# Spreading the C rows of a state-space layer with a float32 product in place of three bfloat16 parts

## What is computed

```
xs = silu(conv(x @ in_w[:DI]))              # DI = 256 channels, 4 taps
dt, B, C = split(xs @ xproj_w)              # rank 8, 16 states, 16 states
dt = softplus(dt @ dt_w + dt_b)
h = exp(dt * A) * h + dt * B * xs           # step by step in time, 16 states per channel
y = sum over states of h * C + D * xs
out = (y * silu(z)) @ out_w
```

## Time and profile before

| | us |
|---|---|
| median of 3 runs | 7244.17 (7243.53 to 7258.09) |
| the profiled execution | 7231.49, span 7229.6 |
| PE busy | 6436.1 (89%) |
| DVE busy | 5332.4 (74%) |
| ACT busy | 4057.1 (56%) |
| POOL busy | 2813.5 (39%) |

### The profile page before, as it was taken

How to read it: one execution, slowest core, us unless ns; L and a number is a source line. 1 busy time by engine, 2 the same in 40 slices (tenths; PEclk the granted TensorE clock), 3 DMA queues, 4 the chain that set the end, 5 groups by cost and what they waited for, 6 DMA issues and landing times. The chain is left out here.

```text
span 7229.6 us, 188705 instructions
## 1 busy us (share of the span) xinstructions
PE 6436.1 (89%) x74428; PEld 3944.6 (55%) x74428; DVE 5332.4 (74%) x8931; ACT 4057.1 (56%) x6024; POOL 2813.5 (39%) x1680
## 2 busy tenths in 40 slices
PE   7989987887797999989999789999899999989998
PEld 5767665444532333333333256666576767666676
DVE  7867576665467999999999856687577777768444
ACT  4556343665447777777777745455344444456433
POOL 3311175332216888888888501164022222221000
PEclk9999988999798999999999899999999999999999
DMA  1000000000101222222222100000000000000000
GB/s 29 0 21 12 8 6 8 3 4 2 15 0 62 76 78 76 80 75 76 73 76 75 47 12 14 22 17 3 12 2 2 2 2 2 2 16 14 1 0 23
DMA packets 115879, 190.00 MB, mean 26 GB/s; under 512 B 38661, under 2 KB 74746, under 8 KB 114970
## 3 DMA queue, kind: packets, MB, share of 16 engines
q1 hardware_dynamic: 112218, 183.47, 8.0%
q10 hardware_dynamic: 3264, 0.54, 0.1%
HBM read 173.87 MB, written 7.98 MB: 25 GB/s over the span
## 5 line engine op out<-in xcount | busy, mean ns | idle before, releaser
L2611 POOL TENSOR_TENSOR m_dBx<-m_dtx,m_Bs 128x1024 f32<-128x1024 f32 x515 | 1166.5, 2284 | 227.1 <-DVE m_hs L2976 185.0
L2976 DVE TENSOR_TENSOR_SCAN m_hs<-m_ps_dA,m_dBx 128x512 f32<-128x512 f32 x1030 | 1203.0, 1212 | 56.6 <-POOL m_dBx L2611 56.0
L2730 PE MATMUL m_ps_y<-m_yc,ident 128*128 128x512 f32 x2060 | 1021.4, 618 | 0.0
L2835 ACT ACTIVATE m_ps_dA<-m_dt,m_A 128x504 f32<-128x504 f32 x1030 | 683.3, 679 | 426.0 <-DVE m_hs L2976 423.4
L2107 POOL TENSOR_TENSOR a_s<-a_s,a_den 128x1024 f32<-128x1024 f32 x128 | 243.8, 1904 | 1123.7 <-DVE a_den L2153 1123.7
L2987 DVE TENSOR_TENSOR m_yc<-m_hs,m_ps_C 128x1024 f32<-128x1024 f32 x515 | 619.3, 1203 | 1.2 <-PE m_ps_C L2711 1.1
L2730 PEld LDWEIGHTS m_ps_y<-m_yc,ident 128*128 128x128 f32 x2060 | 350.0, 189 | 357.2 <-issue 357.2
L2711 PEld LDWEIGHTS m_ps_C<-m_parts,m_sel 48*128 48x128 bf16 x516 | 47.7, 92 | 567.7 <-DVE m_yc L2987 421.4
L2711 PE MATMUL m_ps_C<-m_parts,m_sel 48*128 48x512 bf16 x516 | 199.7, 387 | 176.4 <-DVE m_yc L2987 176.2
L636 POOL TENSOR_TENSOR c_kbd<-c_kf,c_hmask 128x1024 f32<-128x1024 f32 x66 | 125.1, 1895 | 503.0 <-ACT c_kf L545 484.9
L2151 DVE TENSOR_REDUCE a_den<-a_s 128x16 f32<-128x1024 f32 x128 | 156.1, 1219 | 207.5 <-ACT a_s L2058 207.5
(11 more groups left out here) (750 smaller groups left out, 15803.9 us busy)
## 6 DMA issues: line engine op xcount, KB each, us to landing
m_Bs<-BC_rows SPq DMA_DIRECT2D x258, 512.0 KB, 3.6
c_kvb<-in_ctxT SPq DMA_DIRECT2D x68, 128.0 KB, 2.1
c_kvb<-in_ctxT SPq DMA_DIRECT2D x17, 256.0 KB, 2.7
out_dram<-X SPq DMA_DIRECT2D x1, 4096.0 KB
BC_rows<-m_low SPq DMA_DIRECT2D x33, 64.0 KB, 2.9
part_rows<-m_split SPq DMA_DIRECT2D x33, 48.0 KB, 1.7
m_parts<-part_rows SPq DMA_DIRECT2D x33, 48.0 KB, 1.7
m_piece<-BC_rows SPq DMA_DIRECT2D x33, 32.0 KB, 1.7
```

The costliest lines, as they stand in the source:

```text
L2611: return nc.gpsimd.tensor_tensor(to, one, other, ALU.mult)
L2730: last = nc.tensor.matmul(ps_y[:, m, :], C.ident[:], of[:, m, :], start=s == 0, stop=s == NS - 1)
L2835: nc.scalar.activation(seqs(ps_dA[:, h % 3, :]), seqs(dt[:, par, m, :]), ACT.Exp, scale=A[:, second, m, s:s + 1]).then_inc(decay, 1)
L2976: nc.vector.tensor_tensor_scan(hs[:, s % HS, m, :], ps_dA[:, (2 * s + m) % 3, :], dBx[:, s % BX, m, :], 0.0, ALU.mult, ALU.add).then_inc(s ...
```

## The change

The C rows stay in SBUF in float32. The product that spreads them takes, as its weights, one column of the identity, read 128 times (a [32, 128] tile with step 0), and as its moving operand the 32 rows of B and C of the low product, which now has two buffers. `split_rows`, `sel`, `pick_row`, `piece`, `rest`, `split`, `parts`, their DMAs through DRAM and their semaphores are gone, and SP stores the 16 rows of B alone. The last pair of groups is taken out of the hardware loop: group 30 is written with PE's `fronts=1` (only one piece of convolution of the group behind group 31), and group 31 runs states 3 to 15 with no preparation of another group, then its gating, projection and addition.

```diff
-        sel = sb("sel", [P, NS, P], BF16)
...
-        low = sb("low", [P, GT])
-        parts = sb("parts", [P, 2, GT], BF16)
-        piece, rest, split = sb("piece", [P, PIECE]), sb("rest", [P, PIECE]), sb("split", [P, 3, PIECE], BF16)
+        low = sb("low", [P, 2, GT])
...
-        LOOPS = ((0, C.NG // 2 - 1), (C.NG // 2, C.NG))
+        LOOPS = ((0, C.NG // 2 - 1), (C.NG // 2, C.NG - 1))
...
-                sp.dma_start(BC_rows[par], low[0:2 * NS, :]).then_inc(rows_stored, 16)
+                sp.dma_start(BC_rows[par], low[0:NS, par, :]).then_inc(rows_stored, 16)
...
             def spread_C(j, s, par):
                 if s == 0:
-                    pe.wait_ge(parts_loaded, j * 16 + 16)
-                nc.tensor.matmul(ps_C[:], sel[0:3 * NS, s, :], parts[0:3 * NS, par, :], start=True, stop=True).then_inc(C_done, 1)
+                    pe.wait_ge(rows_low, j + 1)
+                one = bc(C.ident[0:2 * NS, NS + s:NS + s + 1], [2 * NS, P])
+                nc.tensor.matmul(ps_C[:], one, low[0:2 * NS, par, :], start=True, stop=True).then_inc(C_done, 1)
...
-            for m in range(NHF):
-                nc.tensor.matmul(ps_y[:, m, :], C.ident[:], yc[:, (AHEAD - 1) % 2, m, :], start=False, stop=True)
+            group(GROUPS - 2, 0, [1, 1, 1, 1], 1)
+            for s in range(AHEAD, NS):
+                if s == SKIPPED:
+                    skip(1, 1)
+                step(GROUPS - 1, s, 1, final=True)
+            project(GROUPS - 1, 1, True)
...
-            def split_rows(j):
-
-                dve.wait_ge(piece_loaded, j * 16 + 16)
-                nc.vector.tensor_copy(split[:, 0, :], piece[:])
-                dve.drain()
-                nc.vector.tensor_tensor(split[:, 1, :], piece[:], split[:, 0, :], ALU.subtract)
-                nc.vector.tensor_tensor(rest[:], piece[:], split[:, 0, :], ALU.subtract)
-                dve.drain()
-                nc.vector.tensor_tensor(split[:, 2, :], rest[:], split[:, 1, :], ALU.subtract).then_inc(split_ready, 1)
...
+            def final_group(i, par):
+                for s in range(AHEAD, NS):
+                    scan(i, s)
+                    weigh(i, s - 1)
+                weigh(i, NS - 1)
+                gated(i, par)
+                add_output(i, True)
```

More of the change, by code:

```diff
@@ L2592, in _ @@
                     group(pair * 2 + par, par)
[L2593 to L2596, removed]
+            for par in range(2):
+                group(GROUPS - 2 + par, par)
         n_prepared = 2
@@ L2651, in _, with group @@
                 state(0, s, 0, True)
-            with pool.Fori(0, C.NG) as pair:
-                for par in range(2):
[L2654 to L2659, removed]
+            def group(i, par):
+                for s in range(AHEAD, NS):
+                    state(i, s, par)
+                    front(i + 1, s, 1 - par)
+                for s in range(AHEAD):
+                    state(i + 1, s, 1 - par)
+            with pool.Fori(0, C.NG - 1) as pair:
+                for par in range(2):
+                    group(pair * 2 + par, par)
+            group(GROUPS - 2, 0)
+            for s in range(AHEAD, NS):
+                state(GROUPS - 1, s, 1)
         @block.tensor
@@ L2703, in step_sizes @@
                 for m in range(NHF):
-                    last = nc.tensor.matmul(bank[m][:], dt_w[rank_rows, m * P:(m + 1) * P], low[rank_rows, :], start=True,
+                    last = nc.tensor.matmul(bank[m][:], dt_w[rank_rows, m * P:(m + 1) * P], low[rank_rows, par, :], start=True,
                                             stop=True)
@@ L2717, in skip, with project @@
                     nc.tensor.matmul(ps_y[:, m, :], diagD[:, m, :], xs[:, par, m, :], start=False, stop=False)
-            def project(i, second):
+            def project(i, second, final=False):
                 pe.wait_ge(y_ready, i + 2)
-                pe.wait_ge(xs_ready, i * NHF + 5)
+                pe.wait_ge(xs_ready, i * NHF + (3 if final else 5))
                 for p in range(TPG):
@@ L2731, in add, with step @@
                 last.then_inc(y_added, 1)
-            def step(j, s, par, between=None):
+            def step(j, s, par, between=None, final=False):
                 rank = DVE_WEIGHS.index(s)
@@ L2737, in step @@
                     spread_C(j, DVE_WEIGHS[rank + 1], par)
-                else:
+                elif not final:
                     spread_C(j + 1, 0, 1 - par)
@@ L2763, in front, with group @@
                     convolve(j + 1, (s - 12) // 2, (s - 12) % 2)
-            def group(i, par, of):
+            def group(i, par, of, fronts=AHEAD):
                 for s in range(AHEAD, NS):
@@ L2772, in group @@
                 for s in range(AHEAD):
-                    front(i + 2, s, par, True, of[2], of[3])
+                    if s < fronts:
+                        front(i + 2, s, par, True, of[2], of[3])
                     step(i + 1, s, 1 - par, (lambda: project(i, of[0])) if s == 0 else None)
@@ L2865, in front @@
                         act.wait_ge(rows_stored, j * 16)
-                    nc.scalar.activation(low[0:64, :], ps_k[0:64, :], ACT.Copy).then_inc(rows_low, 1)
+                    nc.scalar.activation(low[0:64, par, :], ps_k[0:64, :], ACT.Copy).then_inc(rows_low, 1)
                 elif s == 7:
@@ L2927, in _ @@
                     group(pair * 2 + par, par, [1, 1, 1, 1])
-            front(GROUPS + 1, AHEAD, 1, True, 1, 1)
+            group(GROUPS - 2, 0, [1, 1, 1, 1])
+            for s in range(AHEAD, NS):
+                state(GROUPS - 1, s, 1, 1)
         @block.vector
@@ L3016, in group, with gated, add_output @@
                 weigh(i + 1, 1)
+                add_output(i, second)
+            def gated(i, par):
+                dve.wait_ge(y_added, i * NS + NS)
+                nc.vector.tensor_tensor(q[:], sz[:, par, :, :], ps_y[:], ALU.mult).then_inc(y_ready, 1)
+            def add_output(i, second):
                 dve.wait_ge(out_done, i + 1)
@@ L3030, in _ @@
                     group(pair * 2 + par, par, True)
-            weigh(GROUPS, AHEAD - 1)
+            group(GROUPS - 2, 0, True)
+            final_group(GROUPS - 1, 1)
 def mamba_join(C, name):
@@ L4062, in constants @@
     c["pick_mean"] = (row[:, None] // S == np.arange(2)[None, :]).astype(np.float32) / S
[L4063 to L4066, removed]
     c["flip"] = np.kron(np.eye(2, dtype=np.float32), np.eye(S, dtype=np.float32)[::-1]).astype(np.float32)
```

45 lines of the change are left out of this document (15 added, 30 removed).

## The result

The changed kernel takes 7435.26 us (median of 4 runs, 7423.72 to 7446.26), the kernel before 7243.89 in the same comparison: a ratio of 1.026, 95% interval 1.0242 to 1.0279. It is slower, and the forecast of 7437 us is 2 us away. The four runs lie at two values, 7424 and 7446; the profiled one is 7446.26 with a span of 7444.5, and why they differ is not shown, though the mean granted clock is 0.959 and 0.960 in the longer two and 0.962 in the shorter.

A forecast was written before the change was run, and what follows sets the result against it. VectorE was taken to bound the kernel, TensorE after the change: 202 (thirty intervals) + 5.8 (first group) - 14.1 (last group) - 1.2 (setup) = +193 us on 7244.2, so 7437 us; eight times in ten 7390 to 7470.

The forecast's parts named there:

- The gaps at C: TensorE around the C product: passes 0.53 us apart, addition 0.52 behind, a state 2.96, with a front 4.68.
- TensorE becomes the bound, the split buys nothing: State-space groups: TensorE needs 64.8 us against VectorE's 57.15, a group 6.75 longer; the split's 0.90 gains nothing.
- The sum of PE's group, 64.8 us: TensorE's work in one group of sixteen states: 63.9 us, plus 0.8 wait and 0.1 idle, 64.8.
- the step sizes: TensorE's step-size products in each group: taken as the same as the low product's 1.86 us, 3.7 together.
- DVE without the split, 57.15 us: VectorE's group once the split is gone: 58.05 - 0.90 = 57.15 us if VectorE stayed the bound.
- Rival C: C product in one pass: a state takes 2.53 us, VectorE sets the pace again, 7201 us; chance 0.05.
- Rival D: POOL's 1.23 us wait stays in series with PE's work: group 66.0 us, whole 7473; chance 0.04.
- Last group, -14.1: Last gating interval and run-out, without fronts for a further group: 58.5 us instead of 72.6, so -14.1.
- The turn of direction and the second loop: Intervals there counted like the others: thirty from gating to gating, each 6.75 us longer, +202 in all.

The follow-up runs named there:

- the full tile: Changed kernel with the C product on 128 rows, the same tile shape as the additions: 7329.78 us, ratio 1.0115.
- C on 64 rows: Changed kernel with the C product on 64 rows instead of 32, so it shares rows with the step-size products: 7488.32 us, ratio 1.0342.
- the filler: Changed kernel with a third, shortened scan of 380 columns on VectorE in state 9 of each group, result unused: 7431.54 us, ratio 1.0256.
- the one bfloat16 part: Changed kernel with C's rows spread by one bfloat16 product of 32 rows, the two smaller parts left out: 7234.13 us, ratio 0.9995.

## Why the prediction was right, point by point

**The gaps at C.** Right: 0.53 within, 0.52 on leaving, 4.68 with a front; and shown to belong to the tile shape, by the full tile, where they are gone, and by C on 64 rows, where they stay.

**TensorE becomes the bound, the split buys nothing.** Right, shown by the filler (0.92 us of work on DVE, no change) and by the one bfloat16 part (group back to 57.96).

**The sum of PE's group, 64.8 us.** Right within 1.1, and the term that was mis-sized is the step sizes, "taken as the same" as the low product, 1.86. They run beside the C product and together take 1.91, where 1.86 and 1.05 had been summed. With C on 64 rows the group is 64.8, the summed value.

**DVE without the split, 57.15 us.** Wrong. The prediction called DVE the bound, saw one wait of 1.23 us for POOL, and left it standing when it took 0.90 off DVE. The wait grows by what is taken off: groups of 57.96 and 58.03 were measured without the split. Rival C was therefore priced at 7201, and the run that came nearest to it gave 7234. Its sum also contradicts itself: a state of 2.53 us lies above the 2.48 at which PE was to stop being the bound, so a group would have been 64.8 - 16 x 0.43 = 57.9 by the prediction's own numbers. Rival D, which kept that wait in series with PE's work, did not come: in the changed kernel no scan between the first and the last gating waits for POOL, and the group is PE's sum.

**Last group, -14.1.** Right: 13.2 less in the changed kernel, 14.8 when made alone. (The terms listed for 58.5 add up to 58.7, so -13.9.)

**The turn of direction and the second loop** were counted like all other groups. That missed some 10 us at the turn. DVE's new taps take 7.17 us there (5.98 before) and the two diagonals 4.06 (0.76 before), both longer by where POOL stands at that moment: the diagonals end at 3248.68 and 3250.99, two of POOL's instructions at 3248.60 and 3250.90. Behind the diagonals PE runs at a granted clock of 0.50 from 3255 to 3265 us, which costs the bound directly (columns as in the windows above):

```profile
3255.00:3260.00 5.00, 5.00 (x7) 1.48 (x6) 4.95 (x5) 3.07 (x5) 4.53 (x3) 0.50 0.10 34
```

In the run with the scan as filler the diagonals take as long, but the clock falls there for some 3 us only (0.66 in one window of 5 us, 1.00 on either side), and that interval is 69.01 us instead of 72.33.

It also missed 21 us in the second loop: 1.9 in each of five pairs, and 11.4 in one at whose turn PE's clock fell as well (0.55 and then 0.50 from 3425 to 3445 us). That the whole came within 2 us of the forecast is therefore luck: the step sizes, counted some 30 us too high, hid the turn and the second loop, counted some 31 too low.

## What to carry to other kernels

When work is taken off an engine that also waits a little in every round, follow the wait's releaser back before counting a gain: if the releaser is a chain that starts ahead of the removed work, the wait grows by what was removed, and the way to a gain is to shorten that chain, here by one operation moved ahead of another engine's result. Where TensorE is near its limit, a product that makes room elsewhere is priced from start to start, with the gap at each change of tile shape. And a long loop's turn should be read in the profile after any edit: the fetches there came and went with where the loop begins.

## What the hardware showed that was not expected

- Two float32 products on different rows of the array overlap: 1.91 us for both, 2.96 when they share rows.
- A small DVE subtraction of two SBUF tensors took 2.3 to 2.4 us beside a working POOL and 0.2 without; the four multiplies of the taps took 7.17 beside it and 1.43 in the stage's set-up, and the two diagonals, with one tensor as input, 4.06 and 0.48 there.
- Forty drains ahead of a loop removed its fetches and 1.9 us from each pair of groups.
- PE's granted clock fell to its lower level after short lacks of work: in the run with the split kept on DVE, PE worked 4.02 and 4.73 us in two windows of 6, and 0.61 and 0.53 were granted in the second and the third.
